# Values of the odd heads from swapped tokens, fewer window copies, and SyncE's norms later, in a transformer on one core

## The chip, the core and the metric

The kernel runs on one core of one Trainium2 chip. The metric is the device time of one execution in microseconds; the median of three runs is compared. The engines are named as the profile names them: PE (TensorE, with PEld for its weight loads), DVE (VectorE), ACT (ScalarE), POOL (GpSimd) and SP (SyncE, which here only issues DMAs; its queue is shown as SPq).

## What is computed

Two blocks run one after the other over a batch of 4 sequences of 512 tokens with 128 features. The part that matters here is the feed-forward place of the first block, which is itself a small transformer of six layers, in fp32:

```
for i in range(DEPTH):                      # 6
    x = attn_layer(shift_tokens(x), Wqkv[i], q_scale[i], k_scale[i], Wo[i]) + x
    x = ffn_layer(shift_tokens(x), ln_g[i], ln_b[i], W1[i], b1[i], W2[i], b2[i]) + x

def attn_layer(x, Wqkv, qs, ksc, Wo):       # 16 heads of 64, windows of 32 tokens
    q, k, v = split(x @ Wqkv); q = l2norm(q) * qs; k = l2norm(k) * ksc; rotary(q), rotary(k)
    out = local_attention(q, k, v)          # each block of 32 queries sees its own and the previous block of 32 keys
    return out @ Wo
```

The other parts (a recurrent layer before it, a relative-position attention and a mixture of experts behind it) are not touched.

## The kernel before

**Units, tiles, parts.** The transformer is cut into 24 units, one for each layer and sequence. A unit has four tiles of 128 tokens, and a tile two parts, one for each eight heads; a part is scored, softmaxed, turned and weighed at once. So there are 96 tiles and 192 parts.

**The order is written out by hand.** `rounds()` lists rounds. A new unit starts every 32 rounds, and what a unit does stands at fixed steps s from its start. Every engine walks the same list and does, in each round, first what the parts have there and then what the units have there, the older unit first. An engine runs its own program strictly in order, so an early instruction that waits holds all that are behind it. Three units overlap: one in its projections (s from 0 to 31), one in its attention (39 to 76), one in its feed-forward layer (80 to 109). Below, "round 28" means a round whose number is 28 modulo 32, as the newest unit counts it; the unit one older is then at s = 60, the next older at s = 92.

**What stands where.** In `unit_tensor` (PE): eight projections of q and k, one every four rounds; the sums of squares in rounds 0, 8, 16 and 24; for each tile i two products of the values, f = 0 and f = 1 (even and odd heads), at s = 29 + 8i and 31 + 8i. In `part_tensor`: the scores (L1211) at step 0 of a part, the turn (L1219) at 5, the weighing (L1229) at 6, the mixing with Wo (L1237) at 9 of every second part, so in rounds 4, 12, 20 and 28. In `feed_tensor`: `center` (L1162) in round 19, `gate0` in round 27, `gate1` in 31, `gate2` in round 0 (all L1180), `up0` in 4. On ACT: the exponentials of a part (L1357, eight of them) at its step 2, the copy of the turned weights (L1363) at 6, the copy of the output (L1368) at 8, the squares (L1293), the copy of the values (L1306), the copy of each gate (L1341) one round after it, and the copy and the square of the centred input (L1334, L1335) in round 20. On DVE: the rotary products (L1421), the scores' scaling and maximum (L1486, L1491), the reciprocal (L1494), the scaling of k by its norms (L1444) at s = 24, 28, 29 and 32, the addition of the mixed output (L1498). On POOL: the sum of squares (L1556), the rotary sums (L1562, L1563), the softmax's scaling (L1577), the low part of the shifted input (L1540, L1542).

**A ring of two PSUM banks.** Banks 6 and 7 are taken in turn by the sums, the transposed norms, the values, the mixings and all of the feed-forward products. `ring_takes` lists who takes a bank in which round, and `ring_take` makes PE wait until the taker before the last has been read out, whoever that is:

```python
def ring_take(c, t, *user):
    k = t.ring[user]
    if k >= 2:
        c.PE.wait_ge(*ring_freed(t, *t.ring_users[k - 2]))
    return ring_bank(c, t, *user)
```

The order in the ring follows from the steps alone. Before, in rounds 19 to 4 it is: center (19), mix, ffn sum (20), value 3/0 (21), value 3/1 (23), spread, sum (24), gate0 (27), mix (28), value 0/0 (29), gate1, value 0/1 (31), gate2, sum (0), mix, up0 (4).

**Values and windows.** A value product has 128 tokens on partitions. ACT copies it into `v_tok`, and SP copies from there into `v_win` (lines 972, 974, 977): for f = 0 the 64 keys of each of the four query blocks on partitions 0 to 63, for f = 1 on 64 to 127. These are ten DMAs a tile, eight for a sequence's first tile: three of 128 KB for each f and two to four of 64 KB. They are issued in `value_windows`, at s = 31 + 8i, behind a wait for the weighing of the tile two before, since they overwrite its windows. ACT's copy of the values waits for the windows of the two tiles before.

**SP's other work.** The norms of k go out to DRAM (L939, s = 15) and come back spread over partitions (L957, four DMAs each at s = 16, 18, 19 and 24); the weights of the next layer are loaded at its last sequence.

Of the kernel before, what the change touches and what calls it, by code (L numbers as in the profile page):

```python
# [726 lines left out]
UNIT_STEPS = 110  # L727
SPLIT_AT = {2: 13, 3: 31, 0: 39, 1: 40, 4: 56, 5: 59}
# [18 lines left out]
def piece(p):  # L747

    kind, g = divmod(p, GROUPS_TF)
    return kind, g, (1 - kind) * INNER + g * 4 * DH  # L750

# [34 lines left out]
def transformer_setup(c, t, scope):  # L786
# [3 lines left out]
    t.xs = [[sb(f"xs{i}_{k}", [P, S], F32R) for k in range(2)] for i in range(2)]  # L790
    t.xf = sb("x_ffn", [P, S])
# [8 lines left out]
    t.vt = [sb(f"v_tok{i}", [P, 2, PAIRS, DH]) for i in range(2)]  # L800
    t.v = [sb(f"v_win{i}", [P, TPB, PAIRS, DH]) for i in range(2)]
# [18 lines left out]
    t.v_in = [Signal(nc, f"tf_v_in{i}", [(n, k) for n in range(i, UNITS_TF * TPB, 2) for k in range(10 if n % TPB else 8)], 16) for i in range(2)]  # L820
# [7 lines left out]
    t.shift_high, t.shift_low = per("shift_high", units, halves), per("shift_low", units, halves)  # L828
    t.tab_turned, t.tab_kept = one("tables_turned", TABLES), one("tables_kept", TABLES)
# [88 lines left out]
def transformer_sync(c, t):  # L918
    SP = c.SP
    for now in rounds():  # L920
        for kind, u, s in now:
# [3 lines left out]
            if b == B - 1 and l + 1 < DEPTH:  # L925
                if s == PART_FIRST + PART * (PARTS - 1) + PART_STEPS - 1:
                    SP.wait_ge(*t.mixed.on((u + 1) * TPB - 1))
                    load_mix(c, t, l + 1)
                if s == FFN_AT["add"]:
                    SP.wait_ge(*t.f_down.on(u))  # L930
                    load_ffn(c, t, l + 1)
                for x, k in enumerate(order()):
                    then, after = (l + 1, x + RAW) if x + RAW < len(SPLIT_AT) else (l + 2, x + RAW - len(SPLIT_AT))
                    if s == SPLIT_AT[k] + 1 and then < DEPTH:
# [5 lines left out]
            if s in SPREAD_AT:  # L940
                norms_wide(c, t, u, SPREAD_AT.index(s))
            i, at = divmod(s - WINDOWS_AT, TILE)
            if 0 <= i < TPB and at == 0:
                value_windows(c, t, u * TPB + i)
    for v_in in t.v_in + t.wide_in:
        SP.wait_ge(*v_in.all())
# [13 lines left out]
def value_windows(c, t, n):  # L960
# [3 lines left out]
    SP, v, vt, v_in = c.SP, t.v[n % 2], t.vt[n % 2], t.v_in[n % 2]  # L964
# [3 lines left out]
    k = 0  # L968
    for f in range(2):
        at = f * 2 * WIN  # L970
        for blk in range(1, TPB):
            SP.e.dma_start(v[at:at + 2 * WIN, blk, :, :], vt[(blk - 1) * WIN:(blk + 1) * WIN, f, :, :]).then_inc(*v_in.by((n, k)))  # L972
            k += 1
# [1522 lines left out]
```

## Time and profile before

| | |
|---|---|
| runs | 2491.49, 2495.09, 2494.8 us; median 2494.8 |
| profiled execution | 2506.7 us, of which its span 2504.8 us |
| PE, PEld, DVE, ACT, POOL busy | 94%, 70%, 69%, 64%, 58% of the span |
| DMA | 204.6 MB, mean 82 GB/s |

The profiled execution is 11.9 us longer than the median of the runs. The transformer takes the stretch from about 130 to 1850 us; one unit takes some 68 us of it. "Idle before, with a releaser" means that an engine stood still until the named instruction of another engine was done. "Issue" means that it waited for nothing that the profile shows.

### The profile page before, as it was taken

To read this page: it belongs to the slowest core of one execution; us is meant where nothing else is said; L and a number is where in the kernel's file an instruction comes from. 1 tells how busy PE (TensorE), PEld (TensorE's weight loads), DVE (VectorE), ACT (ScalarE), POOL (GpSimd) and SP (SyncE) were. 2 spreads that over 40 slices of the span, in tenths; PEclk is the share of its full clock that TensorE was granted. 3 is DMA by queue.
4 is the path that set the end of the run, shared out by engine and by line. 5 is a ranking of instruction groups with operands and counts; after the bars stand their busy time and mean duration, and the time that the engine had idled before them with its cause. 6 is when DMAs were issued, how large, how long until landed. Compare 5 with 4: busy or idle time off the path is not lost.

```text
span 2504.8 us, 121652 instructions
## 1 busy us (share of the span) xinstructions
PE 2354.9 (94%) x53677; PEld 1748.5 (70%) x53677; DVE 1717.0 (69%) x3393; ACT 1597.2 (64%) x5036; POOL 1451.3 (58%) x1408
## 2 busy tenths in 40 slices
PE   9958999999999999999999999999888999999967
PEld 8836777777777777677777777777645666666657
DVE  4477788777888888787788788887335555555534
ACT  3226777777777787777777778777625454545422
POOL 1166667656676676566666677665117656656307
PEclk9969999999999999999999999999979999999978
DMA  4013333433333334333343333333216222222136
GB/s 91 15 33 86 79 83 94 97 80 83 91 93 95 82 83 103 83 92 87 80 96 90 80 92 87 87 87 87 54 30 177 49 48 48 48 48 48 31 97 249
DMA packets 230208, 204.60 MB, mean 82 GB/s; under 512 B 133687, under 2 KB 155464, under 8 KB 229552
## 3 DMA queue, kind: packets, MB, share of 16 engines
q1 hardware_dynamic: 225296, 190.91, 30.5%
q8 instruction: 422, 6.91, 1.2%
q0 software_dynamic: 2208, 5.58, 0.7%
q14 instruction: 106, 0.87, 0.1%
q10 hardware_dynamic: 2176, 0.33, 0.1%
HBM read 86.05 MB, written 15.70 MB: 41 GB/s over the span
## 4 chain that ended last, share of the span: by engine, by line
PE 66%; DVE 12%; SPq 6%; ACT 5%; issue 5%; POOL 4%; DMA 3%; POOLq 0%; ACTq 0%; DVEq 0%
PE psum L1211 7%; PE psum L1959 5%; PE psum L1237 5%; PE psum L1229 5%; PE psum L1938 4%; PE psum L1111 4%; PE psum L1944 3%; PE psum L1113 3%; PE psum L1112 3%; PE psum L1993 3%; PE psum L1983 3%; ACT p L1357 3%; SPq L972 3%; PE psum L1188 2%; PE psum L1219 2%
## 5 line engine op out<-in xcount | busy, mean ns | idle before, releaser
L1357 ACT ACTIVATE p<-p,stat 128x64 f32<-128x64 f32 x1536 | 512.4, 336 | 47.2 <-DVE stat L1491 44.9
L1577 POOL TENSOR_TENSOR p<-p,inverse 128x512 f32<-128x512 f32 x192 | 200.2, 1043 | 456.5 <-DVE inverse L1494 452.2
L1211 PE MATMUL psum<-kT,qT 32*32 32x64 f32 x24576 | 305.5, 224 | 25.8 <-issue 24.2
L2092 DVE TENSOR_REDUCE largest<-psum 128x1 f32<-128x512 f32 x256 | 165.0, 687 | 228.0 <-PE psum L1944 228.0
L1211 PEld LDWEIGHTS psum<-kT,qT 32*32 32x32 f32 x24576 | 264.1, 103 | 75.3 <-issue 74.3
L1357 ACT ACTIVATION_READ_ACCUMULATOR p<-p,stat 128x1 f32 x1536 | 288.6, 188 | 0.0
L1421 DVE SCALAR_TENSOR_TENSOR rotated<-psum,scales,rotary 128x512 f32<-128x512 f32 x384 | 270.8, 742 | 25.8 <-ACT sq L1293 25.8
L1556 POOL TENSOR_TENSOR squares<-sq 128x512 f32<-128x512 f32 x192 | 245.3, 1278 | 44.3 <-ACT sq L1293 43.8
L1293 ACT ACTIVATE sq<-psum 128x512 f32<-128x512 f32 x384 | 213.7, 582 | 57.3 <-PE psum L1113 54.6
L1229 PEld LDWEIGHTS psum<-pT,v_win 64*64 64x64 f32 x12288 | 198.6, 136 | 64.7 <-issue 45.9
L1111 PE MATMUL psum<-xs,wqkv_high 128*128 128x512 f32 x384 | 205.7, 536 | 23.2 <-DVE rotated L1421 22.9
L2014 ACT ACTIVATE w_by_key<-psum 128x512 f32<-128x512 f32 x128 | 76.4, 597 | 230.1 <-PE psum L1959 230.1
L1229 PE MATMUL psum<-pT,v_win 64*64 64x32 f32 x12288 | 220.1, 221 | 2.8 <-ACT pT L1363 1.8
L1237 PEld LDWEIGHTS psum<-oT,wo 128*128 128x128 f32 x1536 | 187.9, 196 | 38.5 <-issue 26.3
L1237 PE MATMUL psum<-oT,wo 128*128 128x128 f32 x1536 | 198.2, 283 | 9.0 <-ACT oT L1368 5.6
L1363 ACT ACTIVATE pT<-psum 128x512 f32<-128x512 f32 x192 | 114.2, 595 | 130.4 <-PE psum L1219 130.3
L1306 ACT ACTIVATE v_tok<-psum 128x512 f32<-128x512 f32 x192 | 113.8, 593 | 101.8 <-PE psum L1113 73.9
L1444 DVE TENSOR_TENSOR kT<-kT,rnorm_wide 128x1024 f32<-128x1024 f32 x96 | 164.0, 1728 | 13.4 <-DMA rnorm_wide<-rnorms 13.3
L2104 POOL TENSOR_TENSOR q_by_head<-q_heads,mask_head 64x256 fp32r<-64x256 f32 x252 | 157.5, 625 | 15.4
L2060 ACT ACTIVATE weights<-psum,largest 128x512 f32<-128x512 f32 x256 | 161.5, 687 | 3.7 <-DVE largest L2092 3.7
L1421 DVE SCALAR_TENSOR_TENSOR kT<-psum,scales,rotary 128x512 f32<-128x512 f32 x192 | 142.3, 741 | 28.2 <-ACT sq L1293 14.4
L1563 POOL TENSOR_TENSOR qT<-qT,rotated 128x512 f32<-128x512 f32 x96 | 157.9, 1645 | 0.0
(351 smaller groups left out, 5402.3 us busy)
## 6 DMA issues: line engine op xcount, KB each, us to landing
v_win<-v_tok SPq DMA_DIRECT2D x576, 128.0 KB
rnorm_wide<-rnorms SPq DMA_DIRECT2D x384, 64.0 KB
v_win<-v_tok SPq DMA_DIRECT2D x336, 64.0 KB
q_rows<-q_rows_all SPq DMA_DIRECT2D x32, 512.0 KB, 4.6
tile_weights<-expert_table SPq DMA_DIRECT2D x23, 512.0 KB, 5.8
wqkv<-L_ffn_Wqkv SPq DMA_DIRECT2D x96, 64.0 KB, 2.2
rel_values<-sq SPq DMA_DIRECT2D x60, 64.0 KB, 2.2
wo<-L_ffn_Wo SPq DMA_DIRECT2D x48, 64.0 KB
```

The lines of the kernel that those rows point to most:

```text
L1111: PE.e.matmul(out, w[0], x[1], start=True, stop=False)
L1211: last = PE.e.matmul(psum[WIN * blk:WIN * (blk + 1), f, out], q[rows, g, half, tok:tok + WIN], k[rows, g, half, tok:tok + 2 * WIN], start= ...
L1229: last = PE.e.matmul(psum[to:to + DH, 2 + o, at:at + WIN], v[rows, blk, 2 * (2 * a + o) + h, :], t.pt[h][rows, 2 * a + o, blk * WIN:(blk + ...
L1237: last = PE.e.matmul(ps[:, 0:P], t.wo[:, e, :], t.ot[e % 2][:, e // 2, :], start=(e == 0), stop=(e == PAIRS - 1))
L1293: A.e.activation(t.sq[half][:, :], c.psum[:, 4 + half, :], ACT.Square).then_inc(*t.squared.by((u, (p, half))))
L1357: last = A.e.activation(p, p, ACT.Exp, bias=t.stat[:, h, 2 * g + f:2 * g + f + 1], accum_out=t.sum[:, h, g, f:f + 1])
L1421: last = V.e.scalar_tensor_tensor(out=rot[x], in0=psum[:, 4 + half, :], scalar=scale, in1=table, op0=ALU.mult, op1=ALU.mult)
L1444: V.e.tensor_tensor(k, k, t.wide[g % 2][:, :].unsqueeze(1).to_broadcast([P, 2, S]), ALU.mult).then_inc(*t.k_scaled.by((u, g)))
L1556: G.e.tensor_tensor(t.sq_both[p % 2][:, :], t.sq[0][:, :], t.sq[1][:, :], ALU.add).then_inc(*t.squares.by((u, p)))
L1577: G.e.tensor_tensor(p, p, t.inv[:, h, :, :].unsqueeze(3).to_broadcast([P, GROUPS_TF, 2, 2 * WIN]), ALU.mult).then_inc(*t.p_scaled.by(m))
L2060: A.e.activation(t.e[n % 4][:, :], c.psum[:, n % 5, :], ACT.Exp, bias=t.mx[n % 4][:, 0:1]).then_inc(*t.exped.by(n))
L2092: V.e.tensor_reduce(t.mx[n % 4][:, :], psum[:, n % 5, :], AX, ALU.max, negate=True).then_inc(*t.largest.by(n))
```

## The change

It does four things.

1. **Swapped tokens.** A copy `x_swapped` of the shifted input has the two halves of 64 tokens of each tile exchanged. ACT makes it of the high part (two copies of 128x256) and POOL of the low part (two more), at `SWAP_AT` = 28. The values of f = 1 are computed from it, so that their tokens lie on the other half of the partitions.
2. **Windows.** ACT copies the values straight into `v_win`, slot 0. The keys of the odd blocks lie there as they are needed; only those of the even blocks are moved, into slot 1, by SP: six DMAs a tile (four for a first tile) of 96 and 32 partitions with 2 KB each. Scores, weighing, norms and mixing take their operands with f exchanged for blocks 2 and 3 (`swapped`); the copy of the norms on ACT becomes three copies. The number and shape of PE's products stays.
3. **The values are later.** `VALUE_FIRST` goes from 29 to 33, so that values stand in rounds 1, 3, 9, 11, 17, 19, 25 and 27. `WINDOWS_AT` goes from 31 to 37. The wait for the weighing of the tile two before moves from SP to ACT's copy of the values. No step of the feed-forward layer moves.
4. **SP's work is later**: the norms go out at 19 (was 15) and come back at 20, 21, 26 and 30, within a round now behind the windows; k is scaled at 24, 28, 29 and 35 (was 32); weight loads are two rounds later.

By the same rule as above, the order in the ring becomes: center, value 2/1 (19), mix, ffn sum (20), spread, sum (24), value 3/0 (25), gate0, value 3/1 (27), mix (28), gate1 (31), gate2, sum (0), value 0/0 (1), value 0/1 (3), mix, up0 (4).

```diff
-VALUE_FIRST, WINDOWS_AT = 29, 31
+VALUE_FIRST, WINDOWS_AT, SWAP_AT = 33, 37, 28
-NORM_AT = {"root0": 17, "out": 15, "root1": 33, "turn": 39, "copy": 39}
-SPREAD_AT = (16, 18, 19, 24)
-SCALE_AT = (24, 28, 29, 32)
+NORM_AT = {"root0": 17, "out": 19, "root1": 33, "turn": 39, "copy": 39}
+SPREAD_AT = (20, 21, 26, 30)
+SCALE_AT = (24, 28, 29, 35)
-SPLIT_AT = {2: 13, 3: 31, 0: 39, 1: 40, 4: 56, 5: 59}
+SPLIT_AT = {2: 13, 3: 31, 0: 39, 1: 40, 4: 60, 5: 62}
...
+def swapped(f, blk):
+
+    return f if blk < TPB // 2 else 1 - f
...
+    w0, w1, w2, w3 = (slice(WIN * w, WIN * (w + 1)) for w in range(TPB))
+    SP.e.dma_start(v[WIN:P, 1, 0, :, :], v[0:P - WIN, 0, 0, :, :]).then_inc(*v_in.by((n, 0)))
+    SP.e.dma_start(v[w1, 1, 1, :, :], v[w0, 0, 1, :, :]).then_inc(*v_in.by((n, 1)))
+    SP.e.dma_start(v[w0, 1, 1, :, :], v[w3, 0, 1, :, :]).then_inc(*v_in.by((n, 2)))
+    SP.e.dma_start(v[w3, 1, 1, :, :], v[w2, 0, 1, :, :]).then_inc(*v_in.by((n, 3)))
+    if n % TPB:
+        SP.e.dma_start(v[w0, 1, 0, :, :], before[w3, 0, 0, :, :]).then_inc(*v_in.by((n, 4)))
+        SP.e.dma_start(v[w2, 1, 1, :, :], before[w1, 0, 1, :, :]).then_inc(*v_in.by((n, 5)))
...
+        if f:
+            PE.wait_ge(*t.swap_high.on(u))
+            PE.wait_ge(*t.swap_low.on(u))
+        tokens = [x[:, i * P:(i + 1) * P] for x in (t.xp if f else xs)]
...
+def swap_halves(t, u, k):
+
+    to, x = (y[:, :].rearrange("p (i a q) -> p i a q", i=TPB, a=2) for y in (t.xp[k], t.xs[u % 2][k]))
+    return [(to[:, :, 1 - a, :], x[:, :, a, :]) for a in range(2)]
...
+    if s == SWAP_AT:
+        if u:
+            A.wait_ge(*t.valued.on((u * TPB - 1, 1)))
+        for to, x in swap_halves(t, u, 0):
+            last = A.e.activation(to, x, ACT.Copy)
+        last.then_inc(*t.swap_high.by(u))
...
-        for m in (n - 2, n - 1):
-            if m >= 0:
-                A.wait_ge(*t.v_in[m % 2].on((m, 9 if m % TPB else 7)))
-        A.e.activation(t.vt[n % 2][:, f, :, 0:DH], ring_bank(c, t, "unit", u, f"v{i}{f}").rearrange("p (h d) -> p h d", d=DH), ACT.Copy).then_inc(*t.v_kept.by((n, f)))
+        if n >= 2:
+            A.wait_ge(*t.weighted.on(2 * (n - 2) + 1))
+        if n >= 1:
+            A.wait_ge(*t.v_in[(n - 1) % 2].on((n - 1, 5 if (n - 1) % TPB else 3)))
+        A.e.activation(t.v[n % 2][:, 0, f, :, :], ring_bank(c, t, "unit", u, f"v{i}{f}").rearrange("p (h d) -> p h d", d=DH), ACT.Copy).then_inc(*t.v_kept.by((n, f)))
```

## Rows read from the trace of the kernel before

**Rows 1.** The page, chain that ended last: its share by engine
```profile
PE 66%; DVE 12%; SPq 6%; ACT 5%; issue 5%; POOL 4%; DMA 3%; POOLq 0%; ACTq 0%; DVEq 0%
```
**Rows 2.** Busy time by engine in one stretch, granted clock, DMA share, GB/s
```profile
250.00:1760.00 1510.00, 1469.56 (x40393) 1103.12 (x40393) 1210.21 (x2377) 1172.16 (x4083) 986.40 (x775) 1.00 0.35 88
```
**Rows 3.** Waits of PE, 250 to 1760: waited for, us, times, longest
```profile
PE psum L1211 <- issue: 20.8, 39, 1.1
PE psum L1111 <- ACT v_tok L1306: 6.2, 6, 2.8
PE psum L1219 <- POOL p L1577: 4.1, 8, 1.0
```
**Rows 4.** Waits of ACT and of DVE for DMAs, the same stretch
```profile
ACT v_tok L1306 <- DMA v_win<-v_tok: 21.5, 15, 4.1
DVE kT L1444 <- DMA rnorm_wide<-rnorms: 11.6, 15, 1.6
```
**Rows 5.** The page, DMA issues: count, KB each
```profile
v_win<-v_tok SPq DMA_DIRECT2D x576, 128.0 KB
v_win<-v_tok SPq DMA_DIRECT2D x336, 64.0 KB
```
**Rows 6.** Groups by line, 250 to 2000: ACT's copy of a 128x512 product
```profile
L1306 ACT ACTIVATE v_tok<-psum 128x512 f32<-128x512 f32 x182 | 107.8, 592 | 95.2 <-PE psum L1113 70.5 <-DMA v_win<-v_tok 24.5
```
**Rows 7.** Timeline, rounds 19 and 20 of one unit: start, us, engine, line
```profile
1097.72 1.12 PE L1162 MATMUL psum<-x_ffn,center 128*128 128x512 f32 x2
1098.68 1.95 PE L1237 MATMUL psum<-oT,wo 128*128 128x128 f32 x16
...
1099.38 0.59 ACT L1335 ACTIVATE sq<-psum 128x512 f32<-128x512 f32 x1
```
**Rows 8.** Timeline, rounds 27 and 28: gate0, mix, ACT's copy of gate0
```profile
1114.11 1.13 PE L1180 MATMUL psum<-sq,w 128*128 128x512 f32 x2
1115.07 1.95 PE L1237 MATMUL psum<-oT,wo 128*128 128x128 f32 x16
...
1115.28 0.69 ACT L1341 ACTIVATE act<-psum,b1c 128x512 f32<-128x512 f32 x1 [1.61 <-PE psum L1180]
```
**Rows 9.** Timeline of PE: a value product begins, and what follows it
```profile
1120.02 0.39 PE L1111 MATMUL psum<-wqkv_low,xs 128*128 128x512 f32 x1
...
1120.72 0.39 PE L1203 MATMUL psum<-maskb,identb 128*128 128x256 bf16 x2
```
**Rows 10.** Timeline of DVE behind the mixing of round 28
```profile
1117.86 4.31 DVE L1444 TENSOR_TENSOR kT<-kT,rnorm_wide 128x1024 f32<-128x1024 f32 x2
...
1125.50 0.69 DVE L1491 TENSOR_REDUCE stat<-p 128x8 f32<-128x512 f32 x1
1126.10 1.22 DVE L1444 TENSOR_TENSOR kT<-kT,rnorm_wide 128x1024 f32<-128x1024 f32 x1
```
**Rows 11.** Timeline, rounds 0 to 4: gate2 to the turn
```profile
1124.55 1.02 PE L1180 MATMUL psum<-sq,w 128*85 128x512 f32 x2
...
1128.04 0.50 PE L1111 MATMUL psum<-xs,wqkv_high 128*128 128x512 f32 x1
...
1128.89 0.67 ACT L1341 ACTIVATE act<-psum,b1c 85x512 f32<-85x512 f32 x1
...
1131.06 2.05 PE L1237 MATMUL psum<-oT,wo 128*128 128x128 f32 x16 [0.28 <-ACT oT L1368]
1133.15 0.66 PE L1219 MATMUL psum<-ident,p 128*128 128x128 f32 x4
```
**Rows 12.** The same two places in the first and the last of 21 units
```profile
309.05 0.68 ACT L1341 ACTIVATE act<-psum,b1c 85x512 f32<-85x512 f32 x1
...
313.73 0.60 PE L1219 MATMUL psum<-ident,p 128*128 128x128 f32 x4
...
1674.85 0.67 ACT L1341 ACTIVATE act<-psum,b1c 85x512 f32<-85x512 f32 x1
...
1679.58 0.66 PE L1219 MATMUL psum<-ident,p 128*128 128x128 f32 x4 [0.28 <-POOL p L1577]
```

More of the change, by code:

```diff
@@ L790, in transformer_setup @@
     t.xs = [[sb(f"xs{i}_{k}", [P, S], F32R) for k in range(2)] for i in range(2)]
+    t.xp = [sb(f"x_swapped{k}", [P, S], F32R) for k in range(2)]
     t.xf = sb("x_ffn", [P, S])
@@ L828, in transformer_setup @@
     t.shift_high, t.shift_low = per("shift_high", units, halves), per("shift_low", units, halves)
+    t.swap_high, t.swap_low = one("swap_high", units), one("swap_low", units)
     t.tab_turned, t.tab_kept = one("tables_turned", TABLES), one("tables_kept", TABLES)
@@ L933, in transformer_sync @@
                     then, after = (l + 1, x + RAW) if x + RAW < len(SPLIT_AT) else (l + 2, x + RAW - len(SPLIT_AT))
-                    if s == SPLIT_AT[k] + 1 and then < DEPTH:
+                    if s == SPLIT_AT[k] + 3 and then < DEPTH:
                         SP.wait_ge(*t.split_low.on((l + 1, k)))
@@ L1210, in part_tensor @@
                         rows = slice(HALF_D * j, HALF_D * (j + 1))
-                        last = PE.e.matmul(psum[WIN * blk:WIN * (blk + 1), f, out], q[rows, g, half, tok:tok + WIN], k[rows, g, half, tok:tok + 2 * WIN],
+                        last = PE.e.matmul(psum[WIN * blk:WIN * (blk + 1), swapped(f, blk), out], q[rows, g, half, tok:tok + WIN], k[rows, g, half, tok:tok + 2 * WIN],
                                            start=False, stop=(half == 1 and g == GROUPS_TF - 1))
@@ L1297, in unit_scalar @@
             A.wait_ge(*t.scores_kept.on((u - 1) * PARTS - 1))
-        A.e.activation(t.rq[u % 2][:, :, :].rearrange("p b r -> p (b r)"), ring_bank(c, t, "unit", u, "rn")[:, 0:P], ACT.Copy).then_inc(*t.rn_kept.by(u))
+        norms = ring_bank(c, t, "unit", u, "rn")[:, 0:P]
+        A.e.activation(t.rq[u % 2][0:H64, :, :].rearrange("p b r -> p (b r)"), norms[0:H64, :], ACT.Copy)
+        pairs = lambda x: x.rearrange("p (b a h f g) -> p b a h f g", b=TPB, a=2, h=2, f=2)
+        for f in range(2):
+            last = A.e.activation(pairs(t.rq[u % 2][H64:P, :, :].rearrange("p b r -> p (b r)"))[:, :, 1, :, 1 - f, :], pairs(norms[H64:P, :])[:, :, 1, :, f, :], ACT.Copy)
+        last.then_inc(*t.rn_kept.by(u))
     i, at = divmod(s - VALUE_FIRST - 1, TILE)
@@ L1549, in unit_gpsimd @@
         shift_gpsimd(c, t, u)
+    if s == SWAP_AT:
+        if u:
+            G.wait_ge(*t.valued.on((u * TPB - 1, 1)))
+        for to, x in swap_halves(t, u, 1):
+            last = G.e.tensor_copy(to, x)
+        last.then_inc(*t.swap_low.by(u))
     p, at = divmod(s - SQUARES_LAG, 4)
```

44 lines of the change are left out of this document (18 added, 26 removed).

## The prediction, as it was put on record

> **What bounds the kernel now.** I read the chain that ended last first [rows 1]: two thirds of it is PE, and SP's queue and the DMAs have under a tenth. Then the busy time of the long middle stretch [rows 2]: PE is busy for 1469.6 of 1510 us at full granted clock, so it stands still for 40 us, and DVE, the next, is busy for 1210. PE's program order is therefore what sets the time; nothing that speeds another engine can give more than these 40 us there, and every microsecond by which PE is made to wait is added to the end. Third, the waits of PE [rows 3]: half of the 40 us are pauses with no cause in the trace, 6.2 us are waits for the copy of the values, 4.1 us waits for POOL's softmax scaling. Fourth, the DMAs' part [rows 4]: ACT's copy of the values waits 21.5 us for windows, and 6.2 us of that reach PE; DVE waits 11.6 us for the spread norms, none of which is in front of a PE instruction in rows 3.
>
> **Windows and SP's queue.** Before, 576 DMAs of 128 KB and 336 of 64 KB [rows 5] move 95 MB. After, 96 tiles take 384 KB each and the 72 that are not first another 128 KB: 46 MB in 528 issues. All of it runs beside PE. What reaches PE is bounded by rows 3: between 0 and 6.2 us. The windows are now wanted eight rounds after their issue and not fourteen, but a round is about 2 us (a unit of 32 rounds takes (1674.85 - 309.05) / 20 = 68.3 us [rows 12]), and the issue no longer stands behind a wait for a weighing. I take the gain at 3 us in the middle and 3 us for start and end of the transformer, where the same wait stands. For the norms, moved behind this, I take 0: their cover is that k is scaled from round 24 on, and if SP were late there, DVE would be late in the chain below.
>
> **The ring: where the gain is lost.** PE may take a bank only when the taker before the last was read out. The steps of the values move, those of the feed-forward layer do not, so some takers get new partners. I went through the new order and looked for takes whose partner is read out in the same round. There are three.
>
> *Value 0/0 in round 1 waits for gate2, taken in round 0.* ACT copies gate2 in round 1, but its part comes first there: eight exponentials. In the unit of rows 11 that copy ends at 1128.89 + 0.67 = 1129.56. PE gets to this place at 1128.04 now. Two value products (rounds 29 and 31) are no longer in front of it, 0.70 us each [rows 9], so it comes at 1126.64 and stands for 2.9 us. Does ACT come earlier then too? No: its exponentials wait for DVE's maximum, and DVE runs without a break behind the mixing of round 28, two scalings of k taking 4.31 us, up to the maximum that ends at 1126.2 [rows 10]. That chain begins at the mixing and moves with PE. From the copy on I add what PE still has to do up to the turn of round 4: value 0.70, then 1131.06 - 0.28 - 1128.04 = 2.74, value 0.70, and 2.09 from the mixing to the turn, in all 6.23 us [rows 9, 11]. The turn comes at 1135.79 in place of 1133.15, a loss of 2.6 us. In the first and the last of 21 units [rows 12] it is 309.73 + 6.23 - 313.73 = 2.2 and 1675.52 + 6.23 - 1679.58 = 2.2. Read the same way, the 21 units give between 0 (where a DMA had already delayed that unit) and 2.7, in the mean 1.9 us. There are 22 such meetings of two units: 42 us. What PE waits for at that turn now, POOL, is hidden behind it and is counted in it.
>
> *The mixing of round 20 waits for center, taken in round 19.* ACT copies and squares it until 1099.38 + 0.59 = 1099.97 [rows 7]. PE is ready for the mixing at 1098.68 now, and with value 2/1 in between at 1099.38. It waits 0.6 us; 22 times, 13 us.
>
> *The mixing of round 28 waits for gate0, taken in round 27.* The copy ends at 1115.97; PE is ready at 1115.07 + 0.70 = 1115.77 [rows 8]. 0.2 us, 22 times: 4 us.
>
> The mixings of rounds 4 and 12 wait for values read out long before. That PE waits for the swapped tokens costs nothing: they are made in round 28 and wanted in round 3, seven rounds later.
>
> **Work added on ACT and POOL.** ACT gets two copies of 128x256 a unit, and in round 28 also the copy of value 3/1, in front of the copy of the turned weights that PE's weighing waits for. A copy of 128x512 takes 0.59 us [rows 6], so that is 0.6 to 1.8 us. PE would wait for it in round 29, but that is in parallel to DVE's longer chain of rows 10. Also the turns of rounds 8 and 24 no longer have a value product in front of them, so POOL's scaling can come last there. Together between 0 and 1.8 us a unit; I take 0.3, near the lower end since both lie beside the 2.9 us that PE stands anyway: 7 us.
>
> **Pauses.** The 20.8 us of pauses in the scores [rows 3] may shrink when PE stands elsewhere: 0 to 20.8, I take 8.
>
> **The sum.** 42 + 13 + 4 + 7 - 6 - 8 = 52 us. Against the profiled execution that is 2506.7 + 52 = 2559; the median of the runs shown is 11.9 us lower, so 2547 us.
>
> **Rivals.**
>
> *Faster.* The values move from the half of eight rounds that holds the mixing to the half that does not, which evens out PE's work between two parts. If the late chains of ACT and DVE catch up through that, the ring's waits vanish, and with them waits of rows 3. It decides if the copy of gate2 ends before PE arrives, over 2.9 us sooner than in rows 11. For it: PE's waits lie in the short half. Against it: DVE's chain in rows 10 starts at a mixing and has no gap. All of PE's idle time is 40 us; half of it gone is 2475 us. The Trainium skill (SBUF — State Buffer, the line under its title) says that engine ports and DMA ports of SBUF cannot contend. By that rule the halved traffic speeds no instruction by itself; no run here shows it yet.
>
> *A short chain.* The scaling of k takes 1.22 us alone and 2.16 in the pair of rows 10, beside POOL's work. If POOL's work shifts away from it, the chain is 1.9 us shorter and the first loss goes. What is left is 13 + 4 + 7 - 6 - 8 = 10: 2505 us.
>
> *A longer chain.* POOL's two swapping copies stand in round 28, right in front of these scalings. A collision costs 2.16 - 1.22 = 0.94 us [rows 10]. One more a unit gives 22 x 0.94 = 21 us, 2568 us; two give 41, 2588 us. For it: POOL's copies are queued just there. Against it: both scalings collide already. The same title of the skill (SBUF — State Buffer, Terms) says that DVE and GpSimd lock one port pair for a whole instruction and that the loser blocks. The slower pair agrees with a wait for part of an instruction; by the rule each further copy of POOL that falls in DVE's gaps adds up to its whole length.
>
> **Chances.** The forecast, 2547, has 0.61. The longer chain has 0.14, the short one 0.12, the faster case 0.13. The range takes in the first three and leaves the faster case and a tail out: 2500 to 2590. A measurement of this kernel tells about 0.2% (5 us) from no change. The forecast and the longer chain are slower by more than that, and 0.07 of the short chain; 0.05 of it lies within. Slower 0.82, within 0.05, faster 0.13.
>
> **What the profile will show.** Right: new waits of PE's value product for ACT's copy of gate2 of 2 to 3 us in most units, and of the mixing for the square (0.6 us) and for gate0 (0.2 us); a unit of about 70.6 us instead of 68.3; hardly any wait of ACT for windows; DMA at about half the traffic. Wrong would be the chain if ACT's copy of gate2 comes soon after the product itself; wrong would be the sum if PE's waits are there but smaller, which would say that DVE's backlog was not bound to the mixing of round 28; and the part on windows would be wrong if ACT now waits for DMAs at the value of round 25 or 26, whose window is behind the spread of the norms.

## The result, and the profile after

The changed kernel takes 2608.6 us (median of 4 runs) against 2493.1 us for the kernel before in the same measurement: ratio 1.0461, interval 1.0443 to 1.0479, so 115.5 us slower. The forecast was 2547 us, slower by 52 us, with a range of 2500 to 2590 us. In a second measurement the ratio was 1.0486 [1.0461, 1.0512]. The profiled execution is 2606.6 us, its span 2604.4 us.

Line numbers have moved: first product L1114, turn L1232, weighing L1243, mixing L1251, gates L1187, up products L1190, sums L1145, scores L1224; ACT's square of center L1367, copies of gates L1373, of the output L1400, of the values L1338 (now straight into `v_win`); DVE's scaling of k L1476, maximum L1523; POOL's squares L1594, softmax scaling L1615. The page's chain by engine answers to [rows 1], its DMA issues to [rows 5]:

```profile
PE 65%; DVE 15%; ACT 10%; POOL 5%; issue 4%; DMA 1%; POOLq 0%; SPq 0%; ACTq 0%; DVEq 0%
...
v_win<-v_win SPq DMA_DIRECT2D x432, 64.0 KB
...
v_win<-v_win SPq DMA_DIRECT2D x96, 192.0 KB
```

SP's queue has left the chain and the DMAs have 1% of it; DVE (15% for 12%) and ACT (10% for 5%) have taken their share. Busy time in a stretch, columns as in [rows 2], and the waits of PE in the same stretch, as in [rows 3]:

```profile
250.00:1850.00 1600.00, 1492.78 (x40004) 1103.31 (x39997) 1215.04 (x2372) 1185.86 (x4139) 1011.07 (x818) 0.98 0.21 54
```
```profile
PE psum L1114 <- ACT act L1373: 31.5, 17, 2.9
PE psum L1232 <- ACT oT L1400: 19.1, 20, 2.0
PE psum L1224 <- issue: 18.7, 37, 1.2
PE psum L1251 <- ACT sq L1367: 12.4, 21, 0.8
PE psum L1114 <- DVE sq L1489: 4.9, 10, 0.6
PE psum L1145 <- POOL squares L1594: 4.9, 5, 1.0
PE psum L1251 <- ACT act L1373: 3.7, 22, 0.2
PE psum L1232 <- POOL p L1615: 3.5, 9, 0.9
```

The three waits of the ring stand there with the sizes forecast: the value product for gate2, the mixing for the square of center, the mixing for gate0. Three things were not forecast: 19.1 us in which the turn waits for ACT's copy of the output, 4.9 us in which a value product waits for DVE's read of the spread norm (L1489), and a granted clock of 0.98 where [rows 2] have 1.00. PE stands for 107 us in 1600, against 40 in 1510.

To compare kernels I use one yardstick beside the ratio: the stretch from the first to the last of the 24 turns of the norms (before L1146, after L1149), which leaves out what stands before and behind the transformer. Here the rows of that line in five kernels, in this order: before, changed, changed in the second measurement, f1_all_three and h1_gates_early (both below). Columns: count, duration in ns (least, median, most), first and last start.

```profile
L1146 PE MATMUL psum<-ident,rnorm x24: 301/328/329, 187.9 to 1752.8; 128*128 128x128 f32 x24
```
```profile
L1149 PE MATMUL psum<-ident,rnorm x24: 327/328/473, 187.2 to 1854.6; 128*128 128x128 f32 x24
```
```profile
L1149 PE MATMUL psum<-ident,rnorm x24: 300/328/330, 185.6 to 1859.1; 128*128 128x128 f32 x24
```
```profile
L1149 PE MATMUL psum<-ident,rnorm x24: 306/329/331, 185.8 to 1788.0; 128*128 128x128 f32 x24
```
```profile
L1149 PE MATMUL psum<-ident,rnorm x24: 327/328/330, 186.7 to 1769.7; 128*128 128x128 f32 x24
```

Before, the stretch is 1564.9 us (68.0 a unit), after it is 1667.4 and 1673.5 us (72.5 and 72.8 a unit). All of the loss is in it: what lies outside is 940 us before and 937 and 941 us after. Each stretch is that of one profiled execution, and such an execution lies up to 12 us beside the median of its kernel (before: 12 us over it, h1_gates_early: 7 us under it), so differences of stretches carry about that error.

### The profile page after: what moved, and what is told of

The parts are those of the page before. It is cut to its first block, busy times and chain, and to the rows that moved or that the text cites. A ratio compares the mean times of both kernels' runs of the same rounds, so it can differ in the third digit from the quotient of the medians.

```text
span 2604.4 us, 121436 instructions
## 1 busy us (share of the span) xinstructions
PE 2385.5 (92%) x53677; PEld 1750.5 (67%) x53677; DVE 1722.9 (66%) x3393; ACT 1621.0 (62%) x5132; POOL 1477.4 (57%) x1456
## 4 chain that ended last, share of the span: by engine, by line
PE 65%; DVE 15%; ACT 10%; POOL 5%; issue 4%; DMA 1%; POOLq 0%; SPq 0%; ACTq 0%; DVEq 0%
PE psum L1224 7%; ACT p L1389 6%; PE psum L1251 5%; PE psum L1997 5%; PE psum L1114 5%; PE psum L1976 4%; PE psum L1243 4%; DVE rotated L1453 4%; PE psum L1982 3%; PE psum L1116 3%; PE psum L1115 3%; PE psum L2031 3%; PE psum L2021 3%; PE psum L1195 2%; PE psum L1232 2%
## 5 line engine op out<-in xcount | busy, mean ns | idle before, releaser
L1615 POOL TENSOR_TENSOR p<-p,inverse 128x512 f32<-128x512 f32 x192 | 200.1, 1042 | 491.4 <-DVE inverse L1526 490.9
L1224 PE MATMUL psum<-kT,qT 32*32 32x64 f32 x24576 | 301.4, 226 | 21.0 <-issue 20.3
L1224 PEld LDWEIGHTS psum<-kT,qT 32*32 32x32 f32 x24576 | 261.3, 104 | 71.2 <-issue 70.4
L1453 DVE SCALAR_TENSOR_TENSOR rotated<-psum,scales,rotary 128x512 f32<-128x512 f32 x384 | 270.8, 742 | 12.4 <-ACT sq L1313 12.4
L1594 POOL TENSOR_TENSOR squares<-sq 128x512 f32<-128x512 f32 x192 | 245.0, 1276 | 43.2 <-ACT sq L1313 42.9
L1243 PEld LDWEIGHTS psum<-pT,v_win 64*64 64x64 f32 x12288 | 200.1, 136 | 68.5 <-issue 47.6
L1114 PE MATMUL psum<-xs,wqkv_high 128*128 128x512 f32 x384 | 211.2, 550 | 21.3 <-DVE rotated L1453 20.6
L1243 PE MATMUL psum<-pT,v_win 64*64 64x32 f32 x12288 | 222.2, 221 | 4.0 <-ACT pT L1395 2.8
L1251 PEld LDWEIGHTS psum<-oT,wo 128*128 128x128 f32 x1536 | 187.2, 197 | 46.9 <-issue 35.6
L1251 PE MATMUL psum<-oT,wo 128*128 128x128 f32 x1536 | 198.0, 283 | 18.9 <-ACT sq L1367 12.9
L1600 POOL TENSOR_TENSOR kT<-kT,rotated 128x512 f32<-128x512 f32 x96 | 123.6, 1287 | 86.5 <-DVE kT L1453 86.5
L2142 POOL TENSOR_TENSOR q_by_head<-q_heads,mask_head 64x256 fp32r<-64x256 f32 x252 | 157.3, 624 | 15.4
L1476 DVE TENSOR_TENSOR kT<-kT,rnorm_wide 128x1024 f32<-128x1024 f32 x96 | 159.2, 1678 | 0.0
L1116 PE MATMUL psum<-xs,wqkv_high 128*128 128x512 f32 x384 | 158.3, 412 | 0.0
```

The source lines that it names most:

```text
L1114: PE.e.matmul(out, w[0], x[1], start=True, stop=False)
L1116: return PE.e.matmul(out, w[0], x[0], start=False, stop=True)
L1224: last = PE.e.matmul(psum[WIN * blk:WIN * (blk + 1), swapped(f, blk), out], q[rows, g, half, tok:tok + WIN], k[rows, g, half, tok:tok + 2 ...
L1243: last = PE.e.matmul(psum[to:to + DH, 2 + swapped(o, blk), at:at + WIN], v[rows, 1 - blk % 2, f, 2 * (2 * a + o) + h, :], t.pt[h][rows, 2 ...
L1251: last = PE.e.matmul(ps[:, 0:P].rearrange("p (x q) -> p x q", x=2), t.wo[:, e, :], mixed_rows(t, e % 2, e // 2), start=(e == 0), stop=(e = ...
L1453: last = V.e.scalar_tensor_tensor(out=rot[x], in0=psum[:, 4 + half, :], scalar=scale, in1=table, op0=ALU.mult, op1=ALU.mult)
```

## The experiments

All ratios are to the kernel before on the same chip. "Stretch" is the yardstick. "Clock lost" is read from a table of windows of 10 us over the stretch: the sum of (1 - granted clock) x 10 us. It is an upper bound of what the clock costs, since half a clock costs nothing while PE stands. 3 to 14 us of it lie in the first 80 us of the stretch in the kernels looked at (7 before, 8 changed).

| kernel | ratio, interval | stretch, us | clock lost, us |
|---|---|---|---|
| before | 1 | 1564.9 | 10 |
| changed (first; f0_after) | 1.0461; 1.0486 [1.0461, 1.0512] | 1667.4; 1673.5 | 34; 31 |
| e1_scale32 | 1.0387 [1.0354, 1.0420] | 1651.6 | 27 |
| e2_gate2_98 | 1.0407 [1.0377, 1.0437] | 1653.1 | 26 |
| e3_center_gate0 | 1.0375 [1.0343, 1.0407] | 1649.0 | 26 |
| g1_no_scale (e2 + e3) | 1.0296 [1.0255, 1.0337] | 1628.3 | 26 |
| f1_all_three (e1 + e2 + e3) | 1.0184 [1.0152, 1.0216] | 1602.2 | 14 |
| e4_old_windows | 1.0476 [1.0450, 1.0502] | 1669.5 | 34 |
| g3_before_scale35 | 1.0091 [1.0061, 1.0121] | 1576.2 | 9 |
| f2_mix10 | 1.0318 [1.0293, 1.0342] | 1634.5 | 20 |
| f3_before_mix10 | 1.0297 [1.0274, 1.0319] | 1626.2 | 34 |
| g2_all_mix10 | 1.0184 [1.0145, 1.0223] | 1602.9 | 20 |
| g4_no_swap | 1.0156 [1.0113, 1.0200] | 1589.0 | 15 |
| h1_gates_early | 1.0129 [1.0107, 1.0151] | 1583.0 | 7 |
| h2_values37 | 1.0116 [1.0092, 1.0140] | 1583.6 | 7 |
| h3_old_gates | 1.0300 [1.0273, 1.0327] | 1637.8 | 41 |
| i1_values37_shift3 | 1.0242 [1.0216, 1.0268] | 1612.7 | 12 |
| i2_gates_swap32 | 1.0080 [1.0055, 1.0105] | 1574.1 | 9 |
| j1_feed_spread | 1.0461 [1.0434, 1.0488] | 1675.2 | 70 |

### One cause at a time

e1, e2 and e3 each undo one suspected cost in the changed kernel:

```
e1  SPREAD_AT = (20, 21, 26, 28); SCALE_AT = (24, 28, 29, 32)    # were 30 and 35
e2  FFN_AT["gate2"]: 98                                          # was 96
e3  FFN_AT "center": 82, "square": 83, "gate0": 90               # were 83, 84, 91
```

> The changed kernel with the last scaling of k back in round 32 (it was moved to 35) and its spread at 28. In the trace of the changed kernel this scaling takes 1.92 us between the scaling of the scores and their maximum in rounds 3 and 4; ACT's exponentials wait 1.1 us for that maximum, and PE's turn of round 8 then waits 0.94 us for ACT's copy of the output. Theory 'scaling of k in the way': 1.0 to 1.3 us a unit come back, 22 to 30 us, so about 2583 us, and the wait of the turn for ACT's copy of the output (19.1 us in all) mostly goes. Rival 'ring only' (the ring's waits and the lost cover are the whole loss): no change, 2604 to 2612 us.

> The changed kernel with gate2 at step 98 (was 96), so that value 0/0 in round 1 has gate1 as its partner in the ring and no longer waits for the copy behind the exponentials. Theory 'ring': the 31.5 us of waits of the value product for ACT's copy of the gate go and most of it is won: 2580 us, 25 to 32 us less than the changed kernel. Rival 'lost cover' (DVE and ACT are late in this stretch whatever PE waits for, so the wait moves to the turn of round 4 or 8): under 10 us, 2600 us or more, with the waits of the turn for POOL grown.

> The changed kernel with center one round earlier (82, its copy and square 83) and gate0 one round earlier (90), so that a score lies between them and the mixings that take the bank behind the next. Theory 'ring': the waits of the mixing for the square (12.4 us) and for gate0's copy (3.7 us) go, 2592 us. Rival 'lost cover': the time goes to the turns of rounds 24 and 0, 2603 us or more.

> The changed kernel itself, unedited, on this chip. Both theories: ratio to the kernel before 1.044 to 1.048, as in its first measurement; a unit of 72.4 us in the trace. If the ratio is nearer to 1.040, the four runs so far lie within 0.3% of it and their single gains are smaller than they look.

> The changed kernel with the three earlier edits at once: k scaled at step 32, gate2 two rounds later, center, its square and gate0 a round earlier. Theory R (each ring wait and the late scaling cost by themselves): the gains add, 0.3 + 0.5 + 0.7 us a unit, so a unit of 70.9 us and a ratio about 1.025. Theory H (the cost is that the two value products and the mixing now stand in the same half of eight rounds, so the short halves starve while the long ones are full): the waits for gate2 and for center go, but turns wait for the copy of o and for the softmax scaling instead; a unit of 71.3 us or more, a ratio of 1.031 or more.

> The changed kernel with gate2 two rounds later and center, square and gate0 a round earlier, the scaling of k left at step 35. The three edits together brought 2.8 us a unit where their single gains add to 1.5 to 1.7. Theory C (one chain: the ring waits hide each other, the scaling adds its own 0.3 us): a unit of 70.1 us, ratio 1.021 to 1.025. Theory S (the scaling at step 35 is what holds the chain up once the ring waits are gone, though removing it alone brought 0.3 us): a unit of 71.2 us or more, a ratio of 1.03 or more. If gains simply add: 71.3 us too, so that the turn of rounds 0 to 4 and the exponentials' wait for DVE have to tell S from that.

Against 1.0461 to 1.0486 for the changed kernel, e1 brings 0.7 to 1.0 point, e2 0.5 to 0.8 and e3 0.9 to 1.1 (a point is 25 us). Their sum is 2.1 to 2.9 points; the three together bring 2.8 to 3.0, more than theory R wanted and much more than theory H. (The single edits and the repeat of the changed kernel come from separate measurements, each with its own runs of the kernel before; each ratio has an interval of about 0.3 point to either side.) e2 and e3 without e1 (g1) bring 1.7 to 1.9, and the scaling of k another 1.1 on top, about as much as alone. So the gains nearly add. Each edit removed its own wait: in e1 the turn's 19.1 us for ACT's copy of the output are gone from the middle of the transformer, in e3 the wait for the square went from 12.4 to 0.8 us, in e2 that for gate2 is gone. But e2 made a new one, since the gate product had covered it:

```profile
PE psum L1145 <- POOL squares L1594: 17.3, 18, 1.9
```

It also brought out a second one: the up product of round 4 takes the bank of value 0/1, which ACT copies in that same round (5.6 us in e2, none in the changed kernel).

**Why the scaling of k costs.** The prediction had treated this step as one of SP's queue. DVE's timeline in the changed kernel, round 3 of a unit: start, us, engine, line.

```profile
1120.28 0.68 DVE L1518 TENSOR_TENSOR p<-psum,rnorm_tok 128x512 f32<-128x512 f32 x1
1120.87 1.92 DVE L1476 TENSOR_TENSOR kT<-kT,rnorm_wide 128x1024 f32<-128x1024 f32 x1
1122.71 0.27 DVE L1530 TENSOR_TENSOR z<-z,psum 128x128 f32<-128x128 f32 x1
1122.91 0.67 DVE L1523 TENSOR_REDUCE stat<-p 128x8 f32<-128x512 f32 x1
```

At step 35 the scaling falls into a round 3, in which DVE has just scaled the scores; their maximum comes a round later and is now behind it. At step 32 it came behind the maximum, as [rows 10] show (1125.50, then 1126.10). ACT's eight exponentials wait for the maximum, its copy of the output is queued behind them, and PE's turn waits for that copy. The rows of ACT and of PE in the same unit:

```profile
1123.62 0.35 ACT L1389 ACTIVATE p<-p,stat 128x64 f32<-128x64 f32 x1 [1.08 <-DVE stat L1523]
...
1127.25 0.58 ACT L1400 ACTIVATE oT<-psum 128x512 f32<-128x512 f32 x1
```
```profile
1127.97 0.63 PE L1232 MATMUL psum<-ident,p 128*128 128x128 f32 x4 [0.94 <-ACT oT L1400]
```

g3 makes this one edit in the kernel before, where there is no wait of the ring:

```
SPREAD_AT = (16, 18, 19, 30); SCALE_AT = (24, 28, 29, 35)        # were 24 and 32
```

> The kernel before with only the last spread and the last scaling of k moved, from steps 24 and 32 to 30 and 35. My prediction took 0 for it. Theory S: up to 1.5 us a unit even without any ring wait, a ratio of 1.01 to 1.02. Theory C: 0 to 0.3 us a unit, a ratio of 1.000 to 1.004.

0.9 point, 23 us (the stretch of its one profile shows 11): the place of one instruction of DVE has a price even without the ring. The chain can be read in ACT's waits for the maximum, from 250 to 1850 us, in this order: before, g3, changed, e1.

```profile
ACT p L1357 <- DVE stat L1491: 38.9, 73, 1.3
```
```profile
ACT p L1357 <- DVE stat L1491: 80.4, 78, 2.0
```
```profile
ACT p L1389 <- DVE stat L1523: 116.4, 106, 2.4
```
```profile
ACT p L1389 <- DVE stat L1523: 91.7, 88, 2.0
```

With step 35 they grow in either kernel, and in g3 it is the mixing that waits for the copy of the output (9.8 us, before 3.7). Theory C had the price too low, both here and in g1. Theory S had this size, but wanted it to be much larger once the ring is free than the 0.7 to 1.0 point of e1, and 1.1 is not.

### The new windows

> The kernel before with all steps of the changed one (values from 33, windows from 37, norms and weight loads later, last scaling of k at 35), but with the old value tokens, ten window copies a tile and no swapped tokens. Theory 'the steps cost it': as slow as the changed kernel or slower, 2600 to 2640 us, since the larger copies now also have to be done within five rounds. Rival 'the added copies on ACT and POOL cost it': well below, 2500 to 2560 us.

> The kernel before, with its ten window copies and unswapped tokens, at all the later steps of the changed one, and with the three edits of h1_gates_early. Beside that run it says what the new windows (less traffic, the value copy without its wait) bring against the swap and the norm copies (13 us by the run without them). If nothing: the same time within 0.3%. If the old windows cost as before, when ACT's waits for them reached PE by 6 us: equal too; a ratio over 0.5% above h1_gates_early's would say that the old windows are dear in this place.

e4 is the kernel before with all later steps and its old windows; h3 is that with the edits of h1_gates_early (below). e4 is as slow as the changed kernel, with the same waits of PE (33.2 us for gate2, 14.6 for the copy of the output, 11.9 for the square) and none of ACT for windows: the later steps are enough for the loss, and neither the swapped tokens nor the new windows are needed for it. But once the ring is free, h3 is 1.7 points slower than h1, which differs by the new windows, the swap and the norm copies. In h3 ACT and PE wait:

```profile
ACT v_tok L1306 <- DMA v_win<-v_tok: 49.0, 19, 3.9
```
```profile
PE psum L1237 <- ACT oT L1368: 31.2, 19, 3.3
```

So the new windows do bring something, some 43 us with the price of swap and norm copies taken off and the clock counted in (clock lost is 41 us in h3, 7 in h1), but only against old windows at these same late steps. Against the kernel before, whose windows have their old places, it is no gain.

### The mixing a round later

My theory H was that the change puts both value products and the mixing into the same half of eight rounds, and that the short halves starve. f2, f3 and g2 (the latter with all three edits) move the mixing behind the turn:

```
PART_AT "mix": 10, "add": 10                                     # were 9
```

> The changed kernel with the mixing and its addition one step later, so behind the turn of the same round and not in front of it: the mixing leaves the half of eight rounds that holds the values and stands in the other one. Nothing is added or left out. Theory H: the halves, now 10 to 12 us and 6 to 8 us from turn to turn, move by 0.9 us towards each other, and with them much of the loss goes: a unit of 70.0 us or less, a ratio of 1.01 to 1.025, and shorter waits of turns for ACT and POOL. Theory R: only the two ring waits of the mixing (for center's square, 12 us, and for gate0, 4 us) go, as when center and gate0 were moved: a unit of 71.7 us, a ratio of about 1.036.

> The kernel before with the same edit, the mixing and its addition one step later: here it moves into the half that already holds the two value products. Theory H: the halves, now nearly even, move apart by 0.9 us each and the kernel loses what the change lost in part: a ratio of 1.01 to 1.025, a unit of 69.0 to 70.0 us, with turns that wait for ACT or POOL. Theory R: nothing but a take of the ring beside it changes, ratio within 1.005.

> The changed kernel with all three edits and the mixing one step later. If the halves matter beside the waits, this takes another 0.7 to 1.5 us a unit: 68.3 to 69.0 us, a ratio of 1.00 to 1.01. If the mixing's place brought 1.35 us a unit only through its two ring waits, nothing is left for it: 69.8 us and a ratio of 1.018. A gain on the kernel before (ratio under 0.998) would need PE's waits for squares and for the softmax scaling to go as well.

In the changed kernel it brings 1.7 points, between the two theories, but on top of the three edits nothing (1.0184 both). So the uneven halves cost nothing by themselves there. The gain of f2 is in its waits: the mixing's for the square and for gate0 (15.4 us in f0) are gone, and so is most of the turn's for the copy of the output (21.5 us in f0, 1.6 in f2), which e1 removes as well; 15.2 us of a new wait of the up product (L1190) for DVE stand against them. In the kernel before, the same edit costs 3 points, which theory R had at under half a point. Its trace shows why:

```profile
PE psum L1219 <- POOL p L1577: 41.3, 34, 2.7
```

In the kernel before, this wait is 7.8 us in the same stretch of time. There the mixing was what PE did while POOL scaled the softmax. The wait's growth of 33 us and 24 us more of clock lost nearly make up the 61 us by which the stretch grew. H is dropped as the cause of this loss; that cover in front of a turn can be worth this much is kept.

### What is left

h1 takes the three gates a round earlier, in place of gate2 later, so that ACT copies gate2 in a round without exponentials:

```
h1  e1's edit; "center": 82, "square": 83, "gate0": 90, "gate1": 94, "gate2": 95
i2  h1 with SWAP_AT = 32                                         # was 28
g4  f1 without the swapping copies and with one copy of the norms
h2  e1's edit; VALUE_FIRST, WINDOWS_AT, SWAP_AT = 37, 41, 32; SHIFT_AT = -2; SPLIT_AT 4: 64, 5: 66;
    the shift waits for the last tile's value product f = 0 and not f = 1
i1  h2 with SHIFT_AT = -3
```

> The changed kernel with all three edits and without the swapped tokens: the second set's values are computed from the unswapped tokens (so the values of that set are not the reference's), the four swapping copies on ACT and POOL are gone and the norms are copied by one instruction and not by three. It measures what that work costs: my prediction took 0.3 us a unit with bounds 0 to 1.8. If it is nothing, 69.8 us a unit and a ratio of 1.018; if it is what keeps this kernel above the one before, 68.4 us and a ratio of 1.00.

> The changed kernel with k scaled at step 32, center and its square a round earlier, and all three gates a round earlier (gate2 in the round before the exponentials and not behind them). With gate2 two rounds later, PE's wait for it had gone but 16 to 19 us of waits for POOL's squares and 5 us at the first up product had come. Stretch from the first to the last turn of the norms: before 1564.9, changed 1667 to 1673, with gate2 later 1602. If those new waits were the price of that edit: 1580 to 1590 and a ratio of 1.007 to 1.012, without a wait of the sums for squares. If they belong to the place of the values itself: 1600 and a ratio of 1.018 as then.

> h1_gates_early with the two swapping copies on ACT and on POOL four rounds later, in round 0 and not in round 28, where POOL also shifts the next unit's tokens: there swap and shift together (0.74 + 1.27 + 1.95 us) put off a softmax scaling and the squares that the sum of round 0 waits for, 16.8 us in all. If so: the waits for squares fall below 8 us, the stretch from 1583.0 to 1572 to 1577, a ratio of 1.005 to 1.009. If not: 1.0129 as before.

> The changed kernel with the values another four rounds later, at steps 37 to 63, windows at 41, swap at 32, splits at 64 and 66, and the shift of the next unit's tokens two rounds later (it needs the value products done); k scaled at step 32; feed-forward steps untouched. Value products then stand again in front of the turns of rounds 0 and 8, and the ring has the partners that it has in the kernel before. Theory P (the loss is all in the phase of the values to parts and feed-forward, and in the scaling): the stretch from the first to the last turn of the norms is 1565 plus at most 13 us for swapping and norm copies, 1560 to 1580, a ratio of 0.998 to 1.007. If the new windows, the swap or the lengthened unit cost by themselves: 1590 or more, a ratio over 1.012; windows now have only four rounds and would show as waits of PE's weighing for DMAs; the late shift would show as a wait of the first projection.

> h2_values37 with the shift of the next unit's tokens a round sooner, at step -3. In h2_values37 the only interval between turns that was over a us longer than in the kernel before was that of rounds 0 to 4 (10.39 against 9.38 us), and there POOL does the shift (2.4 us) between its softmax scaling and the rotation of q. If that is the cause: the stretch from the first to the last turn of the norms falls from 1583.6 to 1562 to 1572, a ratio of 0.998 to 1.005. If it is the swap or the norm copies that make it late: no change, ratio 1.01.

h1 brings 0.55 point over f1, a bit less than expected; the wait for squares stays (16.8 us), so it was not only the price of e2. The other waits of PE that h1 has and the kernel before has not, or has shorter, are 8.6 us of the weighing for ACT's copy of the turned weights (1.8 before) and 7.4 and 5.7 us at two more pairs of the ring: value 3/0 for DVE's read of the spread norm, and up0 for ACT's copy of value 0/1 (before, 6.2 us of the value product for v_tok). POOL's timeline in h1, round 28 to 30, shows what puts the squares off:

```profile
1125.56 0.74 POOL L1586 CAST x_swapped<-xs 128x256 fp32r<-128x256 f32 x2
1126.63 1.27 POOL L1572 TENSOR_TENSOR xs<-z,xs 64x512 fp32r<-64x512 f32 x1 [0.32 <-ACT xs L1292]
1127.97 1.95 POOL L1574 TENSOR_TENSOR xs<-z,xs 64x511 fp32r<-64x511 f32 x1
1131.27 1.04 POOL L1615 TENSOR_TENSOR p<-p,inverse 128x512 f32<-128x512 f32 x1 [1.34 <-DVE inverse L1526]
1132.27 1.27 POOL L1594 TENSOR_TENSOR squares<-sq 128x512 f32<-128x512 f32 x1
```

The swap stands in front of the shift and ahead of the squares. With it in round 0 (i2) that wait falls to 9.4 us and the ratio to 1.008; the two intervals all but touch, so the gain is between 0 and 1 point (i2's profiled execution, from which its stretch is, was the shortest of six, 12 us under their median). Leaving the swapping and norm copies out (g4; its values of the odd heads are then wrong) brings 0.3 point over f1, within the error. h2 gives the values the old phase to parts and feed-forward layer with the new windows; its 1.0116 is the same as h1's, where 1.007 was the most I expected. Its waits are others: 21.3 us of the turn for POOL's softmax scaling (7.8 before) and 30.7 us of pauses in the scores (22.9 before), but none for squares. i1 was to mend its late shift and made it worse: the shift now waits for the value product of the same round, and POOL's softmax scaling is queued behind it. A row of POOL and one of PE's waits in i1:

```profile
1148.73 1.27 POOL L1572 TENSOR_TENSOR xs<-z,xs 64x512 fp32r<-64x512 f32 x1 [4.91 <-ACT xs L1292]
```
```profile
PE psum L1232 <- POOL p L1615: 53.7, 39, 1.8
```

That expectation missed in sign. No version beat the kernel before; i2 is the nearest.

### A wait can cost more than its length

j1 was to take two more waits of i2 away:

```
"spread": 87, "scale": 88, "up0": 101, "up1": 102                # were 88, 89, 100, 101
```

> i2_gates_swap32 with the spread and the scaling of the feed-forward norm a round earlier (steps 87 and 88) and the first two up products a round later (101 and 102). In the trace of i2 the value product of round 25 waits 7.0 us for DVE's read of the spread and the up product of round 4 waits 6.2 us for the value copy. If each wait is a cost by itself and the ring's new order makes no other: the stretch from the first to the last turn of the norms 1574 to 1561 us, a ratio of 1.002 to 1.004. If waits only pass on to the next link, 1.008 as before. A version faster than the kernel before (under 0.998) would need more than the two waits: chance 1 in 10.

The first wait went. But up2 in round 8 takes the bank of up1, as it did before; up1 now stands in round 6 and not in round 5, and DVE reads it in round 7, behind the products of a rotation and the scaling of a part's scores (in the unit shown below it ends at 1134.26 us, and up2 starts at 1134.31). The pair of the ring is an old one, its two members have come a round nearer, and the ratio goes from 1.008 to 1.046. The wait's row, the place in one unit, and windows of 1 us over it (first column the window, then its length, the busy times of PE, PEld, DVE, ACT and POOL, the granted clock, DMA share, GB/s):

```profile
PE psum L1190 <- DVE act L1496: 54.5, 21, 2.6
```
```profile
1131.09 0.63 PE L1232 MATMUL psum<-ident,p 128*128 128x128 f32 x4
1134.31 1.48 PE L1190 MATMUL psum<-sq,w 128*85 128x512 f32 x2 [2.59 <-DVE act L1496]
1134.84 1.38 PE L1114 MATMUL psum<-xs,wqkv_high 128*128 128x512 f32 x1
```
```profile
1133.00:1134.00 1.00, 0.00 (x0) 0.00 (x0) 1.00 (x3) 0.00 (x0) 0.92 (x1) 1.00 0.00 0
...
1136.00:1137.00 1.00, 1.00 (x4) 0.33 (x2) 0.57 (x1) 1.00 (x7) 0.00 (x0) 0.50 0.00 0
```

After it stood still, PE was granted half the clock, 1.2 GHz in place of 2.4, while it was fully busy again. The stretch grew by 101 us. Waits at this line grew by 46 us (54.5 against 6.2 + 2.5 in i2) and clock lost by 61, more than 101 together: the value product's wait of 7.0 us is gone, the pauses of the scores are 4 us shorter, and part of the slow clock falls into the waits themselves. The same in the changed kernel, where PE had waited for gate2:

```profile
1185.76 0.50 PE L1114 MATMUL psum<-wqkv_low,xs 128*128 128x512 f32 x1 [2.04 <-ACT act L1373]
...
1188.00 2.05 PE L1224 MATMUL psum<-kT,qT 32*32 32x64 f32 x128
...
1191.42 3.11 PE L1251 MATMUL psum<-oT,wo 128*128 128x128 f32 x16
```
```profile
1184.00:1185.00 1.00, 0.00 (x0) 0.00 (x0) 0.90 (x4) 1.00 (x8) 0.00 (x0) 1.00 0.00 0
...
1188.00:1189.00 1.00, 1.00 (x75) 1.00 (x79) 0.00 (x0) 0.98 (x3) 0.93 (x2) 0.50 0.00 0
...
1194.00:1195.00 1.00, 1.00 (x10) 1.00 (x10) 1.00 (x1) 0.00 (x0) 1.00 (x2) 1.00 0.65 184
```

The mixing took 3.11 us in place of 1.95 [rows 7], the scores 2.05 in place of 1.48. Not each wait does this: behind the first 80 us of the changed kernel's stretch PE stands 43 times for 0.9 us or more, and the clock falls at 11 places. But each of the 11 falls begins between 0.3 us before and 1.6 us behind the end of such a wait (0.94 to 2.91 us long, eight times that for gate2), and in j1 each of 26 begins during such a wait or within 1.8 us of its end. The Trainium skill (TensorE: Matmul & The Clock Gate, Part 1) says that the gate follows how busy the engine has been; by that rule the clock falls behind waits, and the trace agrees.

## Why the prediction was wrong, step by step

The direction was right, the size was less than half of it, and the time fell outside the range. I take the stretch in the second measurement: 108.6 us over the kernel before, 21 of them clock lost (31 less 10).

| step of the prediction | forecast | found | from |
|---|---|---|---|
| three ring waits | 59 | 52 | f0 to g1 (45.2) and f1 to h1 (19.2), less 12 of clock |
| SP's norms and the scaling at 35 | 0 | 14 | g1 to f1 (26.1), less 12 of clock |
| all the rest: added work, other pairs of the ring, lost cover, windows, pauses | 7 - 6 - 8 = -7 | 21 | h1 against before (18.1), plus 3 of clock |
| TensorE's clock | none | 21 | sums of windows |
| sum | 52 | 108 | |

The split depends on the order in which the edits are undone: the scaling alone (e1) gives 22 us of stretch, 18 without clock, where g1 to f1 gives 14. The last row but one is the least certain. By medians h1 is 29 us slower than the kernel before and not 18, since the two profiled executions lie on opposite sides of theirs; the rest is then about 32 us. The clock's row is an upper bound.

**What bounds the kernel: right.** PE's order set the time, and each wait put in front of it came out at the end.

**The ring: right, place by place.** The mixing waits 12.4 us for the square (forecast 13) and 3.7 us for gate0 (forecast 4). The value product waits 31.5 us for gate2 in the trace where a loss of 42 us was forecast. That the three come to 52 in all leans on edits that also changed their neighbours: e2 alone took the wait away and gave much of it back to the squares.

**"There are three": not all.** The prediction looked for takers whose partner is read out in the same round. By the same rule value 3/0 (round 25) has the spread norm, which DVE reads in round 25, and up0 (round 4) has value 0/1, which ACT copies in round 4. The first cost 4.9 us in the changed kernel (7.0 in its repeat); the second cost nothing until other waits were gone (5.7 us in h1, 6.2 in i2).

**"For the norms, moved behind this, I take 0": wrong.** This is the first failed step. I read the move as one of SP's queue and asked only if the spread norms would be there in time; they were, and DVE's waits for them [rows 4] are gone. But the fourth scaling of k moved with them from step 32 to 35, and I did not look up what stands next to it on DVE. [Rows 10] had the answer: behind the maximum at 1125.50, not in front. e1, g1 to f1, and g3 put it at 0.7 to 1.1 points, 18 to 28 us.

**The gains: wrong.** ACT's waits for windows did vanish, and the traffic went from 88 to 54 GB/s, but 6 + 8 us did not come. The pauses in the scores are 18.7 us where they were 20.8. The value's wait in [rows 3] was in part replaced by the 4.9 us for the spread norm.

**Added work: too small a term.** With the swap in round 28 POOL's squares come late (16.8 us of waits in h1, 9.4 with the swap in round 0). i2 and g4 give between 0 and 1 point for swap and norm copies together. What remains, about 0.8 point in i2 and more in h2, I can't put down to one cause: the traces show where PE waits in each (above), but no run takes these waits away one by one. h2, which has the old phase, loses as much, so it doesn't come from the values' new phase alone.

**No term for the clock: the second failed step.** A wait was priced at its own length. In the changed kernel clock lost rose from 10 to 31 and 34 us, each fall behind the first 80 us at a wait; with most waits taken away it was back at 7 (h1).

**The rivals.** The "longer chain" had POOL's swap as the cause and 2588 us at most: the cause plays a small part, the size was still too low. The "faster" and the "short chain" cases did not come: ACT's copy of gate2 stayed late. The rule that SBUF's engine and DMA ports cannot contend (Trainium skill, SBUF - State Buffer, the line under its title) changed nothing, and the traces agree: DVE's scaling of the scores takes 681 ns on average at 88 GB/s before and 679 ns at 54 GB/s after.

**What the profile was to show.** A unit of 70.6 us: it is 72.5. "Wrong would be the sum if PE's waits are there but smaller" was the wrong alarm: they were there, and the sum failed by what stood beside them.

## What to carry to other kernels

When a step of one engine is moved, look up every instruction that moves with it, and for each the neighbours on its own engine in the new round: one that lands between two links of a chain can delay the chain in every unit (here a scaling of 1.9 us cost 0.8 to 1.2 us a unit). In a shared ring of buffers a new order makes new pairs and brings old ones nearer; list all pairs whose first is read out in the round in which the second is taken, or in the round before it, before and after each edit, also after a repair. Price a wait of PE at more than its length, since the clock can fall behind it: in j1, 46 us of added waits came with a stretch longer by 101 us. It is no fixed factor: in the changed kernel 67 us more of standing came with 21 to 24 us more of clock lost.

## What the runs showed of the hardware

Waits of PE of 2.0 and 2.6 us (the changed kernel, j1), in a stretch where it was otherwise busy, were followed, in the two places shown, by 6.8 and 3.4 us at a granted clock of 0.50, with PE at work throughout. Behind the first 80 us of the stretch there are 2 such places in the kernel before, 11 in the changed kernel and 26 in j1 (clock lost 70 us in the whole stretch), each of them at a wait of PE of 0.9 us or more; most waits of that length in the changed kernel (32 of 43) have no fall of the clock.
